# The last layer of a graph and transformer network on one core: attention units overlapped by one, weights loaded beside the norms, and norm rows in two vector operations

## What is computed

```python
x = x + L0_gnn(layernorm(x)); x = x + L0_ffn(layernorm(x)); x = x + L1_gnn(layernorm(x))
z = layernorm(x)                                  # no scale, no offset
n = ln(z, g1, b1)                                 # a second norm, with scale g1 and offset b1
scores = sigmoid(n @ Wr + br)                     # one number per token
idx = top_k(-scores, 188)                         # 15% of the 1250 tokens
q, k, v = n @ Wq + bq, n @ Wk + bk, n @ Wv + bv   # 12 heads of 64
ctx = softmax(q k^T / 8) v                        # only the 188 picked rows are needed
attn_out = ctx @ Wo + bo
mix_out = (n + scores * pooled) @ Wm + bm         # pooled: mean of n weighted by scores
h = z + where(picked, attn_out, mix_out)
n2 = ln(h, g2, b2)
x = x + h + gelu(n2 @ W1 + bf1) @ W2 + bf2
```

## Time and profile before

| | us |
|---|---|
| three runs, median | 3301.93 |
| three runs, lowest and highest | 3301.04 and 3302.32 |
| the profiled execution: time | 3298.07 |
| the profiled execution: span from first to last instruction | 3296.3 |
| TensorE busy in the span | 2732.4 |
| VectorE busy | 2093.9 |
| ScalarE busy | 1294.1 |

### The profile page before, as it was taken

The page is one execution under the profiler, slowest core; times in us unless marked ns, Lnnn a source line. Parts: engine busy times, 40 slices in busy tenths (PEclk is TensorE's granted clock), DMA queues, the critical chain, the costliest instruction groups (busy, mean ns, idle before and its releaser), DMA issues. The chain is left out here.

```text
span 3296.3 us, 35744 instructions
## 1 busy us (share of the span) xinstructions
PE 2732.4 (83%) x12628; PEld 2026.0 (61%) x12629; DVE 2093.9 (64%) x3230; ACT 1294.1 (39%) x1728; POOL 301.7 (9%) x148
## 2 busy tenths in 40 slices
PE   7867966888566966997999997997999599998869
PEld 3546962233236853555999985996888455565544
DVE  6755998999843545982889887506768760124351
ACT  1563217988410001113888872215556310013210
POOL 0000000000045851000000003300000000000002
PEclk9987558999868988998999997998999699999969
DMA  1556526101026545424532313425334310000031
GB/s 65 149 157 156 163 86 250 47 31 47 29 59 213 190 148 197 171 80 139 153 101 82 100 52 134 163 76 174 123 121 145 124 37 29 29 30 1 1 85 47
DMA packets 173005, 344.95 MB, mean 105 GB/s; under 512 B 28821, under 2 KB 94813, under 8 KB 172091
## 3 DMA queue, kind: packets, MB, share of 16 engines
q1 hardware_dynamic: 127924, 253.57, 25.2%
q10 hardware_dynamic: 35968, 73.97, 6.3%
q0 software_dynamic: 8960, 15.41, 1.9%
HBM read 259.93 MB, written 82.91 MB: 104 GB/s over the span
## 5 line engine op out<-in xcount | busy, mean ns | idle before, releaser
L1260 PE MATMUL rg1a_acc<-rg1a_values,rg1a_high 125*125 125x193 f32 x2400 | 407.5, 334 | 40.3 <-DMA rg1a_values<-values_dram 20.2
L1260 PEld LDWEIGHTS rg1a_acc<-rg1a_values,rg1a_high 125*125 125x125 f32 x2400 | 403.0, 192 | 45.0 <-issue 22.6
L1421 PE MATMUL gat_acc<-far_u,gat_ft 125*65 125x512 f32 x720 | 287.4, 540 | 76.2 <-DVE far_u L1485 75.8
L1302 DVE TENSOR_TENSOR rg1a_high<-rg1a_high,rg1a_lowb 125x625 f32<-125x625 f32 x240 | 194.3, 810 | 118.6 <-ACT rg1a_lowb L1278 103.6
L1421 PEld LDWEIGHTS gat_acc<-far_u,gat_ft 125*65 125x65 f32 x720 | 94.3, 142 | 265.6 <-issue 171.0
L1056 PE MATMUL rg_out<-rg_w,rg_hT 128*125 128x384 f32 x720 | 234.3, 489 | 0.0
L1942 PE MATMUL rg2a_acc<-rg2a_value_part,rg2a_wts_part 125*125 125x512 f32 x600 | 206.3, 344 | 28.5 <-DVE rg2a_wts_part L1661 18.9
L1277 ACT ACTIVATE rg1a_high<-rg1a_rows,rg_ks 125x625 f32<-125x625 f32 x240 | 196.3, 818 | 70.2 <-PE rg1a_acc L1260 40.6
L1943 PE MATMUL rg2a_acc<-rg2a_value_part,rg2a_wts_part 125*125 125x512 f32 x600 | 206.8, 345 | 0.0
L1944 PE MATMUL rg2a_acc<-rg2a_value_part,rg2a_wts_part 125*125 125x512 f32 x600 | 205.2, 342 | 0.0
L1056 PEld LDWEIGHTS rg_out<-rg_w,rg_hT 128*125 128x125 f32 x720 | 135.7, 189 | 97.5 <-issue 1.8
(11 more groups left out here) (433 smaller groups left out, 5205.0 us busy)
## 6 DMA issues: line engine op xcount, KB each, us to landing
rg2a_values<-values_dram SPq DMA_DIRECT2D x90, 384.0 KB, 3.3
rg1a_values<-values_dram SPq DMA_DIRECT2D x240, 96.0 KB, 1.9
rg_mask<-far_dram SPq DMA_DIRECT2D x60, 312.5 KB, 3.4
moe_raw<-in_L_ffn_w SPq DMA_DIRECT2D x16, 1152.0 KB, 6.8
gat_rows<-rows_dram SPq DMA_DIRECT2D x12, 1250.0 KB, 5.7
rg1a_rows<-shift_dram SPq DMA_DIRECT2D x24, 625.0 KB, 6.8
relw_chunk<-in_L_gnn_W ACTq DMA_DIRECT2D x36, 384.0 KB, 3.1
sorted_dram<-gat_zeros SPq DMA_DIRECT2D x30, 384.0 KB, 10.9
```

The lines of the kernel that those rows point to most:

```text
L1260: last = pe.matmul(tile_of(u, d), wts[i % HB][:, d * TP:(d + 1) * TP], stream[i % 4][:, :], start=first and d % per_bank == 0, stop=final, ...
L1302: dve.tensor_tensor(high[i % HB][:, 0:w], high[i % HB][:, 0:w], lowb[i % LB][:, 0:w], op=ALU.max).then_inc(max_done, 1)
L1421: last = pe.matmul(acc[h % 2][0:WIDTH, b, 0:c1 - c0], ft[:, t, h, :], wts[i % HB][:, c0:c1], start=(t == 0), stop=(t == NT - 1))
```

## The change

**Norms.** In `normalize_twice` VectorE does two operations a tile in place of three, straight from x: (x - mean) * g1, then * both scales + b1. Two small operations (`zn_offset`, `zn_both_inv`) make what these need. `z` is made by ScalarE, one activation of 125x768 a tile, ahead of the two copies of the tile's turn. In `normalize` with scale and offset (`n2`) the three operations become two in the same way.

**Loads.** Wk is loaded by SyncE in `normalize_twice`, behind g1 and b1 and ahead of the saving of x. In `pick_tokens` bk is then loaded ahead of Wr and br. The feed-forward weights and the saved x are loaded in the block of the norm of `n2`, the biases ahead of the matrices.

**Attention.** TensorE turns unit i in two halves of five transposes, with five products of the context of unit i - 1 behind each half. The two halves share one bank `att_turn`; the context has a bank of its own, `att_ctx`. `scores` has no wait left. ScalarE does the exponential of unit i + 1 between the two copies of unit i. VectorE copies the context of unit i - 3 ahead of the maximum of unit i.

```diff
-                    link(dve.tensor_scalar(dst[:, t, :], src[:, t, :], mean_var[:, t, 0:1], std_inv[:, t:t + 1],
-                                           op0=ALU.subtract, op1=ALU.mult))
-                    link(dve.tensor_tensor(dst[:, t, :], dst[:, t, :], affine[0:TP, 0, :], op=ALU.mult))
-                    dve.tensor_tensor(dst[:, t, :], dst[:, t, :], affine[0:TP, 1, :], op=ALU.add).then_inc(rows_done, 1)
+                    link(dve.scalar_tensor_tensor(out=dst[:, t, :], in0=src[:, t, :], scalar=mean_var[:, t, 0:1],
+                                                  in1=affine[0:TP, 0, :], op0=ALU.subtract, op1=ALU.mult))
+                    dve.scalar_tensor_tensor(out=dst[:, t, :], in0=dst[:, t, :], scalar=std_inv[:, t:t + 1],
+                                             in1=affine[0:TP, 1, :], op0=ALU.mult, op1=ALU.add).then_inc(rows_done, 1)
...
+            keys.load(sp)
             for a, b in SPLIT:
                 sp.dma_start(keep_in[a:b, :, :], x[a:b, :, :]).then_inc(kept, 16)
...
+            act.wait_ge(offset_done, 1)
             for t in range(NT):
+                act.activation(z[:, t, :], x[:, t, :], ACT.Identity, bias=offset[:, t:t + 1],
+                               scale=std_inv[:, 0, t:t + 1]).then_inc(z_done, 1)
                 act.wait_ge(turned, t + 1)
...
             def scores(i):
-                if i >= 2:
-                    pe.wait_ge(ctx_out, i - 1)
...
+            def turn(i, half):
+                if half == 0:
+                    pe.wait_ge(scaled, i + 1)
+                if 2 * i + half:
+                    pe.wait_ge(turned_out, 2 * i + half)
...
             scores(0)
             for i in range(len(units)):
                 if i + 1 < len(units):
                     scores(i + 1)
-                context(i)
+                for half in range(2):
+                    turn(i, half)
+                    if i:
+                        context(i - 1, half)
+            for half in range(2):
+                context(len(units) - 1, half)
...
+            exponential(0)
+            for i in range(len(units)):
                 for half in range(2):
                     act.wait_ge(turned, 2 * i + half + 1)
                     if i >= 2:
                         act.wait_ge(ctx_made, i - 1)
                     act.activation(probsT[i % 2][:, half * 5:half * 5 + 5, :].rearrange("p t q -> p (t q)"),
-                                   turn_ps[half][:, 0:5 * QT], ACT.Copy).then_inc(turned_out, 1)
+                                   turn_ps[:, 0:5 * QT], ACT.Copy).then_inc(turned_out, 1)
+                    if half == 0 and i + 1 < len(units):
+                        exponential(i + 1)
```

More of the change, by code:

```diff
@@ L451, in _ @@
                     sp.dma_start(affine[:, i, :], rows_of(v, P, 0, D)).then_inc(affine_in, 16)
+            if ahead:
+                ahead.load(sp)
         @block.vector
@@ L517, in _, with normalize_twice @@
                     other.finish(pe)
-def normalize_twice(g, x, z, n, nT, gamma, beta, keep_in, eps=1e-5):
+def normalize_twice(g, x, z, n, nT, gamma, beta, keep_in, keys, eps=1e-5):
     with ExitStack() as ctx:
@@ L532, in normalize_twice @@
         square = s.sb("zn_square", [TP, 2, NT])
+        both_inv = s.sb("zn_both_inv", [TP, NT])
+        offset = s.sb("zn_offset", [TP, NT])
         affine = s.sb("zn_affine", [P, 2, D])
@@ L2485, with __init__, load, pick_tokens @@
 DH = D // HEADS
-def pick_tokens(g, n, nT, wr, br, wk, bk, wm, keep, picks, picksT, picked_nT, score_rows, kT, w_sb):
+class KeyWeights:
+    def __init__(self, s, wk, w_sb):
+        self.wk, self.w_sb, self.w_in = wk, w_sb, s.sem("pick_wk_in")
+    def load(self, sp):
+        sp.dma_start(self.w_sb[:, :, :], self.wk.rearrange("(c p) f -> p c f", p=128)).then_inc(self.w_in, 16)
+def pick_tokens(g, n, nT, wr, br, wk_in, bk, wm, keep, picks, picksT, picked_nT, score_rows, kT, w_sb):
     with ExitStack() as ctx:
@@ L2755, in attend_picked @@
         score_ps = [s.ps(f"att_score{i}", [128, 3, 512]) for i in range(2)]
-        turn_ps = [s.ps(f"att_turn{i}", [TP, 512]) for i in range(2)]
+        turn_ps = s.ps("att_turn", [TP, 512])
+        ctx_ps = s.ps("att_ctx", [128, 512])
         flat = [x[0:QT, :, :].rearrange("p a b -> p (a b)") for x in score_ps]
@@ L2788, in scores, with context @@
                 last.then_inc(scored, 1)
-            def context(i):
-                q, h = units[i]
-                pe.wait_ge(scaled, i + 1)
-                for half in range(2):
-                    if i >= 1:
-                        pe.wait_ge(turned_out, 2 * (i - 1) + half + 1)
-                    for k in range(5):
-                        t = half * 5 + k
-                        last = pe.transpose(turn_ps[half][:, k * QT:(k + 1) * QT], probs[i % 2][:, t * TP:(t + 1) * TP],
-                                            g.ident[0:QT, 0:QT])
-                    last.then_inc(turned, 1)
-                pe.wait_ge(turned_out, 2 * i + 2)
-                at = slice(h % 2 * DH, h % 2 * DH + DH)
-                for t in range(NT):
-                    last = pe.matmul(score_ps[i % 2][at, 0, 0:QT], v[:, t, h * DH:(h + 1) * DH],
+            def turn(i, half):
[3 more added lines that the diff above has]
+                    pe.wait_ge(turned_out, 2 * i + half)
+                for k in range(5):
+                    t = half * 5 + k
+                    last = pe.transpose(turn_ps[:, k * QT:(k + 1) * QT], probs[i % 2][:, t * TP:(t + 1) * TP],
+                                        g.ident[0:QT, 0:QT])
+                last.then_inc(turned, 1)
+            def context(i, half):
+                q, h = units[i]
+                at = slice(h % 2 * DH, h % 2 * DH + DH)
+                pe.wait_ge(turned_out, 2 * i + half + 1)
+                if half == 0 and i:
+                    pe.wait_ge(ctx_out, i)
+                for t in range(half * 5, half * 5 + 5):
+                    last = pe.matmul(ctx_ps[at, 0:QT], v[:, t, h * DH:(h + 1) * DH],
                                      probsT[i % 2][:, t, :], start=(t == 0), stop=(t == NT - 1))
-                last.then_inc(ctx_made, 1)
+                if half:
+                    last.then_inc(ctx_made, 1)
             scores(0)
@@ L2885, in _, with exponential @@
         def _(act):
-            for i in range(len(units)):
+            def exponential(i):
                 act.wait_ge(topped, i + 1)
@@ L3016, in mixed_layer @@
             nT = si.sb("n2T", [128, KC, N])
+            weights = FeedWeights(si, g, w1, bf1, w2, bf2)
             with ExitStack() as inmost:
                 n2 = Scope(g, inmost).sb("n2", [TP, NT, D])
-                normalize(g, "n2_ln", z, n2, nT, g2, b2, stats=g.row_stats)
-            feed_forward(g, z, nT, w1, bf1, w2, bf2, out)
+                normalize(g, "n2_ln", z, n2, nT, g2, b2, stats=g.row_stats, ahead=weights)
+            feed_forward(g, z, nT, weights, out)
 def build(nc, io, out):
```

72 lines of the change are left out of this document (42 added, 30 removed).

## The result

The changed kernel takes **3343.61 us** (median of 4 runs, 3342.85 to 3351.71), the kernel before 3302.08 us beside it (4 runs, 3301.04 to 3302.32). The ratio is 1.0133, with an interval from 1.0119 to 1.0146: the change makes the kernel 41.5 us **slower**. The forecast was 3242.5 us, with a range up to 3254. The time lies 101 us above the forecast, and close to the 3348 us of the fourth rival, "TensorE at 1.2 GHz in all of the attention".

What follows compares the result with a forecast made beforehand. VectorE was taken to bound the norms, TensorE the attention and token picking, with waits for weights. 6.2 + 11.0 - 0.2 + 30.6 + 5.6 + 6.2 = 59.4 us off 3301.93 gave 3242.5 us, 8-in-10 range 3234 to 3254.

Steps and rivals of the forecast that it cites:

- the fourth rival: Attention: TensorE at 1.2 GHz in all of it, 10.2 us a round, 3348 us in all; chance 0.02.
- Norms: Both norms: two VectorE operations a tile repeating after 2.02 us, saving 6.2 us in the first and 5.6 in the second.
- Key weights: Picking of tokens: with the weights loaded early, the 11.0 us wait for the first key product goes, less 0.2.
- the two values for bk: Picking of tokens: bk lands 0.34 or 3 us later, costing 0 to 0.8 us; 0.2 was taken.
- Feed-forward weights: Feed-forward: with weights loaded during the second norm, the 6.2 us wait ahead of the first product goes.
- The round of the attention: Attention: TensorE is the bound, both waits go, and a round takes 5.4 us (5.15 to 5.7) instead of 6.50.
- the 30.6 of the sum: Attention's whole gain in us: 24.2 from rounds, 6 from clock drops, 1.6 at the start, less 1.2 at the end.
- The clock: Attention: low-clock losses go with the waits, gaining 6 us at four drops, with 2 lost at the start.
- The first rival: Attention: four to six drops of the clock remain, 6 to 9 us stay, about 3250 us; chance 0.13.
- the second: Rival in the attention: the chain through the exponential, not TensorE, sets a round of 6.6 us, 3273 us; chance 0.02.
- The early loads: Rival: late bk, late saving of x and ScalarE behind in the norm cost 3 to 5 us, 3247; chance 0.06.
- The spread: Behind the attention: the output product and the spread were taken as the same work, with no gain or loss.

Runs made afterwards that it cites:

- e1: The changed kernel with the attention of the kernel before, so only norms and early loads changed: 3278.72 us, ratio 0.9933 against the kernel before.
- e4: The changed kernel with four unused products put in TensorE's wait ahead of the attention's first transposes: 3236.04 us, ratio 0.9807.
- e3: The changed kernel with the ten context products of a unit in one piece between the two halves of the transposes: 3240.7 us, ratio 0.9822.
- e2: The kernel before with only the new attention: 3383.59 us, ratio 1.0254 against the kernel before.
- e6: e4 with VectorE taking the maximum of unit 12 five times, so that TensorE waits once: 3306.0 us, ratio 1.0011 against the kernel before.
- e8: The changed kernel with 26 unused transposes in TensorE's wait at the attention's start: 3352.53 us, ratio 1.0145 against the kernel before.
- e10: The changed kernel with two unused products in TensorE's wait at the attention's start: 3355.24 us, ratio 1.0157 against the kernel before.
- e5: The changed kernel with six unused products once, ahead of unit 12's transposes: 3306.95 us, ratio 1.0015 against the kernel before, one of eight runs left out of the ratio.

## Why the prediction was wrong, point by point

**Norms: right.** Predicted 6.2 and 5.6 us, measured 6.8 and 5.8. The pair of operations repeats after 1.98 to 1.99 us, where 2.02 had been worked out. z took ScalarE 1.03 us, just above the bound of 1.01, which was drawn in proportion from 625 columns. It stayed hidden, as z and copies are 1.89 us a tile, under VectorE's 1.99. SyncE's saving of x didn't end the block.

**Key weights: right.** Predicted 11.0 less 0.2 for bk. The first key starts 0.02 us into its block, and the block is 10.3 us shorter (10.4 in e1), half a us less than the 10.8 of the sum. Of the two values for bk, the lower one was nearer: the scores began 4.16 us into the block, as they had before.

**Feed-forward weights: right.** 6.2 predicted; the first product is at the block's start.

**The round of the attention: right in its work, wrong in its price.** TensorE is the bound, both waits are gone, and the other engines are in time, as was worked out. At full clock the round is 5.61 us (e4), inside 5.15 to 5.7. In e3 and e4 the attention is 26.3 and 28.3 us shorter than before (167.5), near the 30.6 of the sum. That sum would have been about right for a clock that stays up, which is what it took for granted but for the start.

**The clock: this step failed.** It was put so: "The other 13 fall on four contexts like the one that took 3.29 in place of 1.84, each just behind the wait for the copies. ... With the waits gone I expect these losses to go", and, for the start, "part of it runs at the lower clock (2 lost)". Both sentences take a low clock for the price of a wait that ends soon after the wait. The rows showed two things, and only one was used. That waits take it down was seen. What brought it back was not asked. The first fall ended in a context in one piece at the low level (3.26 us), and each of the four later ones covers such a context, of 3.29 to 3.40 us; at the end of that piece the clock came back each time. The change cuts just this piece in two and puts transposes between, and it keeps the 3.39 us wait that takes the clock down. Once down, it didn't return in any of the 22 rounds: 22 times 10.51 in place of 5.4 are 112 us, where the sum had 6 gained at the drops and 2 lost at the start. The attention took 251.6 us against the 136.9 that the sum makes of it (167.5 less 30.6). That the piece in one is what brings the clock back is shown from both sides: put together again, it does so at the end of the first such piece (e3), and in the five kernels that were still low at the end of the attention (the changed one, e2, e6, e8, e10) the clock rose inside the last unit's context or at most 0.6 us behind it. Why such a piece does it and its halves with transposes between do not, the runs don't show. Two of the signs that the prediction named for its own fall were there: scores after more than 6 us, and a clock under 0.9.

**The rivals.** The fourth was the case, with the right mechanism and nearly the right size: 10.2 us a round against 10.51, 3348 us against 3343.61. Its chance of 0.02 was set by "the mean of 0.94 with even more idle time". That mean belongs to an order which had the cure in it, so it said nothing of one that didn't. What spoke for the rival, the turns of the norms with 1.51 us for six and the Trainium skill's rule on transposes (TensorE: Matmul & The Clock Gate, Part 4), was in the text, and weighed too little. (The transposes were 1.33 of the 5.44 us of a unit's work, a quarter and not the fifth that is stated there.) The first rival (drops remain) and the second (the chain sets the round) didn't come about: at the full clock there is neither. The early loads got in nobody's way.

**The spread** was taken as unchanged. It was 7.6 us shorter in the changed kernel, by a fall of the clock that took place before and not after. Without this the profiled runs would differ by 52 us. As shown above it isn't part of the change.

## What to carry to other kernels

When a change cuts TensorE's long pieces of products into short ones with transposes between them, ask of each wait ahead of it what will bring the clock back, and not only whether the waits get fewer. A few unused products in the one wait that starts such a phase (here four, some 3.7 us of cover) can be worth more than the whole reordering, and in this kernel keeping the ten products in one piece did nearly as much; in these runs transposes in that place didn't serve, and neither did half the products. If a mean clock is used to judge an order, look at the mixture right behind each fall and at the piece at which it rises, since the mean belongs to the old order alone.

## What the runs showed of the hardware that was not expected

- The same mixture of work on TensorE ran at full clock or at half of it for as long as it lasted, by the level that it met. It was busy for 243.33 of 245 us at a clock of 0.50 in the changed kernel, and for 135.94 of 138 us at 1.00 in e4. Being busy all the time did not bring it back.
- In this mixture one wait of 3.39 us, of 1.47 us (e10), or 3.06 us of transposes with 0.40 and 0.65 us of waiting (e8) came before a fall for the rest of the phase. The fall can come late: in e8 and e10 the first transposes still ran at the full clock, and it fell 2.4 to 2.5 us behind the wait. In the old order waits of 0.65 and 0.42 us twice a unit led to only four short falls in 24 units.
- It came back at the end of ten context products in one piece (e3, 13.7 us after the fall), in the burst of six wide products (e5, 5.3 us into it), and in or just behind the last unit's context, the only one in one piece, in the five kernels of the new order that were low until then.
- The work ahead of the first norm of the last layer, which is the same in all kernels, took 2579.8 to 2594.4 us in the profiled runs. Five microseconds in a late block are therefore better read from the block's own length than from the time of the run.
